# Expert layers: sorted rows turned by tile, up weights stationary in a copied buffer, routing weight applied in the sum

## The chip, the cores and the metric

The kernel runs on one core of a Trainium2 chip. The metric is the device time of one execution in microseconds (us). The kernel before takes 1945.29 us, the median of three runs (1944.04 to 1947.86).

## The reference

One block of four residual layers on x of 4 x 1024 tokens with 128 channels, all float32:

```
x = x + attn_a(layernorm(x))     # 16 heads of 8 channels
x = x + moe(layernorm(x))        # 8 experts, top 2
x = x + attn_b(layernorm(x))     # gated delta rule, a scan over tokens
x = x + moe(layernorm(x))        # the same experts again

moe(x): probs = softmax(x @ gate_w)          # 128 x 8
        top_w, top_i = top_k(probs, 2); top_w = top_w / sum(top_w)
        for e in range(8):
            h = silu(x @ w1[e]) * (x @ w3[e])   # w1, w3: 128 x 256
            out += route[:, e] * (h @ w2[e])    # w2: 256 x 128
```

The change is to the moe alone, which the kernel runs twice.

## The kernel before

`moe` sorts the 4096 tokens by their pair of experts (28 pairs) and works through the sorted rows in tiles of 128. A *pass* is one tile with one expert. A tile meets two experts and more where a pair ends inside it, so that 2 x 32 + 27 = 91 passes (`NPASS`) always suffice; those not needed get addresses of a zero weight. One layer goes as follows.

**Routing** (DVE, with small tables made by POOL). `find_best` takes each token's two experts, `count_pairs` counts the pairs, `place_all` gives each token its place in the sorted order (`slot`), and `plan` gives each pass the first row of its tile (`row_at`) and the place of its expert's weights in SBUF (`w_at`). ScalarE meanwhile writes the normalised rows into `xr` (L1144). Each row of `xr` has 144 numbers: 128 channels, the routing weight of each of 8 experts, and the token's number.

**Scatter.** POOL issues 32 indirect DMAs (L1064), each of which writes 128 rows of `xr` to their sorted places in DRAM (`expert_rows`). They wait for `xr`, for the weights and for `slot`. `plan` runs beside them.

**The 91 passes.** SP loads the tile of each pass from DRAM (L1025), one DMA of 72 KB for each pass, into one of eight buffers (`xin`). Each engine has its own order, written out by hand, and waits on semaphores:

- PE, for pass n: `up(n)` (L1095) is one float32 matmul with the turned tile stationary and 512 columns of w1 and w3 moving; its output has tokens on the partitions. Then PE loads a register with the weights' address for the next pass (L1117). `turn_h(n-2)` (L1102) turns the two halves of the product, `turn_rows` (L1088) in every other pass turns the tiles of the next two passes, and `down(n-3)` (L1110) is two matmuls with w2 moving, summed in PSUM.
- ScalarE: `silu(n)` (L1154), and `take_h(n-2)` (L1159), which copies the turned product to SBUF.
- DVE: `product(n)` (L1311) multiplies silu, the other half and the routing weight; in every other pass `take_rows` (L1295) copies two turned tiles to SBUF and `own_weights` (L1301, L1304) picks the weights out of the rows; `add(n-3)` (L1319) loads a register with the tile's column (L1315) and adds the pass's output to `y`.

In the trace a float32 matmul shows as two records of LDWEIGHTS and two of MATMUL, a transpose as one of each.

**Return.** POOL issues 32 indirect DMAs (L1071) that add `y` to the residual in DRAM. Tile t's waits until min(2t + 29, 91) passes are added. After the first moe the residual is loaded back and its statistics are taken; the second moe writes the kernel's output, and nothing follows it.

Of the kernel before, what the change touches and what calls it, by code (L numbers as in the profile page):

```python
# [11 lines left out]
BF16 = mybir.dt.bfloat16  # L12
ALU = mybir.AluOpType
# [866 lines left out]
COL_W, COL_ID, ROW = P, P + E, 144  # L880
PIECE = 4
NPIECE = NT // PIECE
NXIN = 8
BACK = 8
WE = 3 * F


def moe(nc, g, ins, scr, phase, layer, norm_next, out=None):

    with ExitStack() as ctx:  # L890
# [11 lines left out]
        first = m.sb("first", [P, NT])  # L902
        lane = m.sb("lane", [P, 1])
        names = m.sb("names", [P, E])
        unit = m.sb("unit", [P, NT * E])
# [14 lines left out]
        slot = m.sb("slot", [P, NT], mybir.dt.uint32)  # L920
# [5 lines left out]
        upper = m.sb("upper", [P, NT, PAIRS])  # L926
        lower = m.sb("lower", [P, NT, PAIRS])
        meet = m.sb("meet", [P, NT, E, E])
        needed = m.sb("needed", [P, NT * E])
        upto = m.sb("upto", [P, NT * E])  # L930
        passed = m.sb("passed", [P, NT * E])
        spot = m.sb("spot", [P, 1])
        tile_no = m.sb("tile_no", [P, 1])
        expert = m.sb("expert", [P, 1])
        none = m.sb("none", [P, 1])
        code = m.sb("code", [P, 2])
        spread = m.sb("spread", [P, 2, P])
        row_at = m.sb("row_at", [P, NPASS], mybir.dt.int32)
        w_at = m.sb("w_at", [P, NPASS], mybir.dt.int32)
        which = m.sb("which", [P, NPASS, E])  # L940
        ids = m.sb("ids", [P, NT, 2], mybir.dt.uint32)
        xin = m.sb("xin", [P, NXIN, ROW])
        mine = m.sb("mine", [P, 2, 2, E])
        scale = m.sb("scale", [P, NPASS])
        xgT = m.sb("xgT", [P, 3, 2 * P])
        gate = m.sb("gate", [P, 3, F])
        hs = m.sb("hs", [P, 3, F])
# [3 lines left out]
        ps_t = m.ps("ps_t", [P, CH])  # L951
        ps_r = m.ps("ps_r", [P, CH])
        ps_g = m.ps("ps_g", [P, CH])
        ps_p = m.ps("ps_p", [P, CH])
        ps_h = [m.ps(f"ps_h{i}", [P, 2, F]) for i in range(2)]
# [9 lines left out]
        s_ids = m.sem("ids_set")  # L965
# [23 lines left out]
        s_hturn = m.sem("h_turned")  # L989
        s_hT = m.sem("hT")  # L990
# [5 lines left out]
        ps_ht = [ps_t, ps_r]  # L996
        ps_up = [*ps_h, ps_p[:, :].rearrange("p (w f) -> p w f", w=2)]
        before, total = ps_p[:, 0:PAIRS], ps_p[:, PAIRS:2 * PAIRS]
        spread_ps = ps_p[:, 2 * P:4 * P]
# [13 lines left out]
        def _(sp):  # L1013
            sp.dma_start(resid_tiles, g.x[:, :, :]).then_inc(s_kept, 16)
            sp.wait_ge(s_scat, landed)
            for n in range(2):
                sp.dma_start(xin[:, n, :], scr.xg[0:P, :]).then_inc(s_load[n], 16)
            sp.wait_ge(s_plan, 1)
            for n in range(2, NPASS):
                if n >= NXIN:  # L1020
                    pair = (n - NXIN) // 2
                    sp.wait_ge(s_gturn, pair + 1)
                    sp.wait_ge(s_mine, pair + 1)
                row = sp.value_load(row_at[0:1, n:n + 1], min_val=0, max_val=(NT - 1) * P)
                sp.dma_start(xin[:, n % NXIN, :], scr.xg[bass.ds(row, P), :]).then_inc(s_load[n % NXIN], 16)  # L1025
                if n == NXIN - 1:
                    sp.dma_start(ids[:, :, :], scr.xg.bitcast(mybir.dt.uint32)[:, COL_ID:COL_ID + 2].rearrange(
                        "(t p) o -> p t o", p=P)).then_inc(s_rid, 16)
# [7 lines left out]
        def _(pool):  # L1036
            pool.iota(rank[:, :], pattern=[[-1, E]], base=E, channel_multiplier=0,
                      allow_small_or_imprecise_dtypes=True).then_inc(s_tables, 1)
            pool.memset(unit[:, :], 1.0).then_inc(s_tables, 1)
            pool.iota(xr[:, :, COL_ID:COL_ID + 1].bitcast(mybir.dt.int32), pattern=[[P, NT], [0, 1]], base=0,  # L1040
                      channel_multiplier=1).then_inc(s_ids, 1)
            pool.memset(xr[:, :, COL_ID + 1:ROW], 0.0).then_inc(s_ids, 1)
# [15 lines left out]

# [1114 lines left out]
```

## Time and profile before

| | |
|---|---|
| runs | 1944.04, 1945.29, 1947.86 us |
| profiled execution | 1948.65 us, span 1946.9 us |
| mean granted TensorE clock | 0.826 |
| busy over the span | PE 68%, DVE 76%, ACT 47%, POOL 17% |
| first moe | from 862.9 us (its first DMA) to its last return DMA at 1082.6 us |
| second moe | from 1720.1 us to the end |
| passes | 925 to 1081 us and 1782 to 1939 us |

The span is the time from the first to the last instruction. The percentages are means over stages of different kinds: the attention fills the first 830 us, the delta rule lies between the two moe layers. For a change to the moe only the stretches of the moe say what it is worth.

### The profile page before, as it was taken

Reading aid. Unit: us, or ns where it says so; the run is one execution under the profiler, and the core shown is the slowest. Engines: PE = TensorE matmul, PEld = TensorE weight load, DVE = VectorE, ACT = ScalarE, POOL = GpSimd, SP = SyncE. Lnnn points to the kernel's source line nnn. Section 1 sums busy time; section 2 is a strip of 40 time slices with the busy share of each in tenths; the row PEclk is TensorE's granted clock in tenths of the full one; section 3 lists DMA queues with packets and bytes.
Section 4 is the critical chain, followed back from the end, with each engine's and each line's share of the span. In section 5 each row is a group of like instructions: output and inputs, shape, how many; then the busy total and the mean of one; then the engine's idle time right before and its main releaser. Section 6 shows DMA issues by size and latency. Waiting matters only on the chain. (4 is left out here: it accounts for less than half of the span.)

```text
span 1946.9 us, 42337 instructions
## 1 busy us (share of the span) xinstructions
PE 1322.8 (68%) x15088; PEld 722.1 (37%) x15088; DVE 1484.1 (76%) x2893; ACT 918.5 (47%) x2025; POOL 328.7 (17%) x330
## 2 busy tenths in 40 slices
PE   4689999999999999960999482000000079923998
PEld 2215555554555555350566242000000024411665
DVE  5698899989998999153566484999999979961665
ACT  4508888888888888951344372001222200030443
POOL 6000000000000000016034100000000045544044
PEclk9859999999999999985899785555555589965999
DMA  3510111111111100031233227610221110012243
GB/s 91 175 46 23 37 30 30 30 30 30 31 39 46 33 3 3 2 109 49 54 62 63 52 106 123 188 44 11 65 66 46 26 49 0 1 57 59 52 67 44
DMA packets 118653, 100.86 MB, mean 52 GB/s; under 512 B 23665, under 2 KB 100018, under 8 KB 118066
## 3 DMA queue, kind: packets, MB, share of 16 engines
q1 hardware_dynamic: 101570, 84.79, 17.0%
q0 software_dynamic: 11264, 8.92, 3.2%
q10 hardware_dynamic: 5616, 4.47, 1.3%
q8 instruction: 124, 2.03, 0.4%
q14 instruction: 79, 0.65, 0.1%
HBM read 55.98 MB, written 31.21 MB: 45 GB/s over the span
## 5 line engine op out<-in xcount | busy, mean ns | idle before, releaser
L727 DVE TENSOR_REDUCE att_negmax<-att_ps_max 128x1 f32<-128x1024 f32 x512 | 620.8, 1223 | 66.1 <-PE att_ps_max L590 37.3
L715 ACT ACTIVATE att_probs<-att_ps_prob 128x512 f32<-128x512 f32 x1024 | 556.3, 595 | 128.8 <-PE att_ps_prob L605 126.4
L590 PE MATMUL att_ps_max<-av_k_op,av_q_op 81*32 81x512 bf16 x4096 | 418.1, 401 | 13.2 <-PEq L104 7.2
L605 PE MATMUL att_ps_prob<-av_q_op,av_k_op 99*32 99x512 bf16 x4096 | 407.7, 382 | 2.9
L625 PE MATMUL att_ps_acc<-att_probs,att_vq 128*32 128x256 f32 x4096 | 313.8, 379 | 0.0
L1942 PE MATMUL out_ps_y<-all_bo_row,all_ones 1*128 1x128 f32 x2 | 0.8, 481 | 372.4 <-PEq L104 372.4
L590 PEld LDWEIGHTS att_ps_max<-av_k_op,av_q_op 81*32 81x32 bf16 x4096 | 112.7, 97 | 145.6 <-DVE att_negmax L727 44.9
L605 PEld LDWEIGHTS att_ps_prob<-av_q_op,av_k_op 99*32 99x32 bf16 x4096 | 108.8, 95 | 145.7 <-ACT att_probs L715 93.8
L625 PEld LDWEIGHTS att_ps_acc<-att_probs,att_vq 128*32 128x32 f32 x4096 | 131.2, 111 | 78.2 <-issue 0.5
L1154 ACT ACTIVATE moe_moe_gate<-moe_moe_ps_h 128x256 f32<-128x256 f32 x122 | 46.7, 383 | 214.1 <-PE moe_moe_ps_h L1095 202.1
L1942 PEld LDWEIGHTS out_ps_y<-all_bo_row,all_ones 1*128 1x128 f32 x2 | 0.5, 304 | 372.7 <-issue 372.7
L1095 PE MATMUL moe_moe_ps_h<-all_w_all,moe_moe_xgT 128*128 x244 | 128.8, 610 | 1.4 <-DVE moe_moe_xgT L1295 1.4
L1319 DVE TENSOR_TENSOR moe_moe_y<-moe_moe_y,moe_moe_ps_y 128x128 f32 x182 | 52.4, 288 | 87.9 <-issue 81.7
L1844 ACT ACTIVATE solve_p<-solve_state,solve_decay 128x32 f32<-128x32 f32 x128 | 45.0, 352 | 155.5 <-DVE solve_state L1828 155.5
L1110 PE MATMUL moe_moe_ps_y<-all_w_all,moe_moe_hT 128*128 x728 | 111.6, 276 | 0.3
L531 POOL CAST att_nm_parts<-att_nm_rows 32x128 bf16<-32x128 f32 x16 | 4.5, 284 | 546.4 <-ACT att_nm_rows L696 546.4
L1110 PEld LDWEIGHTS moe_moe_ps_y<-all_w_all,moe_moe_hT 128*128 128x128 f32 x728 | 95.5, 191 | 1.5 <-issue 1.5
L1295 DVE COPY moe_moe_xgT<-moe_moe_ps_g 128x256 f32<-128x256 f32 x92 | 38.2, 415 | 68.2 <-PE moe_moe_ps_g L1088 68.2
L1937 POOL TENSOR_TENSOR out_qS<-b_q,out_St 128x1024 f32<-128x1024 f32 x32 | 75.4, 2355 | 65.9 <-DVE out_St L2046 65.9
L1088 PE MATMUL moe_moe_ps_g<-all_ident,moe_moe_xin 128*128 128x128 f32 x182 | 36.3, 280 | 68.8 <-DMA moe_moe_xin<-expert_rows 68.7
L1311 DVE SCALAR_TENSOR_TENSOR moe_moe_hs<-moe_moe_gate,moe_moe_scale,moe_moe_ps_h 128x256 f32<-128x256 f32 x122 | 58.3, 478 | 21.9 <-ACT moe_moe_gate L1154 21.7
L2046 DVE TENSOR_TENSOR_SCAN out_St<-b_a,out_ps_k 128x1024 f32<-128x1024 f32 x32 | 73.2, 2287 | 1.1
(276 smaller groups left out, 2067.0 us busy)
## 6 DMA issues: line engine op xcount, KB each, us to landing
moe_moe_xin<-expert_rows SPq DMA_DIRECT2D x182, 72.0 KB
av_k_op<-terms_k SPq DMA_DIRECT2D x48, 216.0 KB
av_q_op<-terms_q SPq DMA_DIRECT2D x144, 72.0 KB
solve_dec_and_windows<-solve_Xw SPq DMA_DIRECT2D x16, 256.0 KB, 3.0
solve_dec_and_windows<-solve_k SPq DMA_DIRECT2D x16, 256.0 KB, 3.7
terms_q<-qkv_parts_q SPq DMA_DIRECT2D x8, 384.0 KB, 2.6
terms_k<-qkv_parts_k SPq DMA_DIRECT2D x8, 384.0 KB, 3.1
all_w_all<-in_f_w SPq DMA_DIRECT2D x24, 128.0 KB, 2.5
```

The lines of the kernel that those rows point to most:

```text
L590: mm = pe.matmul(ps_max[c * STRIP:(c + 1) * STRIP, a % 2, k * CH:(k + 1) * CH], q_op[s][0:R_ALL, h, at:at + STRIP], k_op[s][0:R_ALL, h, k ...
L605: mm = pe.matmul(ps_prob[c * STRIP:(c + 1) * STRIP, j % 2, :], k_op[s][0:R_END, h, at:at + STRIP], q_op[s][0:R_END, h, half * CH:(half + 1 ...
L625: mm = pe.matmul(ps_acc[half][32 * h:32 * h + 32, cols], vq[:, s % 2, kt, VW * h:VW * h + 32], probs[:, (GH * v + h) % PROBS, cols], start ...
L715: act.activation(probs[:, j % PROBS, :], ps_prob[:, j % 2, :], ACT.Exp).then_inc(s_exp, 1)
L727: dve.tensor_reduce(negmax[:, s % 2, a:a + 1], ps_max[:, a % 2, :], AX.X, ALU.max, negate=True).then_inc(s_maxed, 1)
L1095: pe.matmul(ps_up[n % 3][:, :, :].rearrange("p w f -> p (w f)"), xgT[:, n // 2 % 3, cols], wall[:, bass.ds(at0, 2 * F)], start=True, stop= ...
L1110: mm = pe.matmul(ps_y[n % 2][:, 0:P], hT[:, n % 3, i * P:(i + 1) * P], wall[:, bass.ds(at0 + (2 * F + i * P), P)], start=(i == 0), stop=(i ...
L1154: act.activation(gate[:, n % 3, :], ps_up[n % 3][:, 0, :], ACT.Silu).then_inc(s_silu, 1)
L1311: dve.scalar_tensor_tensor(out=hs[:, n % 3, :], in0=gate[:, n % 3, :], scalar=scale[:, n:n + 1], in1=ps_up[n % 3][:, 1, :], op0=ALU.mult, ...
L1319: dve.tensor_tensor(tile, tile, ps_y[n % 2][:, 0:P], ALU.add).then_inc(s_sum, 1)
L1937: pool.tensor_tensor(qS[:, e % 2, :], q[:, b * S:(b + 1) * S], St[:, e % 2, :], ALU.mult).then_inc(s_qS, 1)
L2046: dve.tensor_tensor_scan(St[:, e % 2, :], a[:, tok], ps_k[e % 2][:, :], 0.0, ALU.mult, ALU.add).then_inc(s_S, 1)
```

## The change

Five things are different in `moe`.

1. SP loads the sorted rows once, all 32 tiles, in seven DMAs of 1, 1, 2, 4, 8, 8 and 8 tiles (`PARTS`) into `xs`, which keeps them all. PE turns each tile once and DVE copies each once (`xgT` keeps all 32).
2. `up` has the weights stationary: four float32 matmuls of 128 columns, with 128 x 128 of w1 or w3 stationary and the turned tile moving. Its output has the 256 inner channels on the partitions, so that the product is already in the form that `down` needs: `turn_h`, `take_h` and `hs` go, and `down` follows two passes behind instead of three. ScalarE copies the weights of pass n+3 into one of three buffers (`wbuf`), at an address that it loads into a register of its own.
3. PE and DVE load two registers with one load (`two_loads`), without a check of the bounds at run time. ScalarE's load has the check.
4. The routing weight is no longer in the product. `add` multiplies by it, from `xs` at a column found by register: its form is now `scalar_tensor_tensor`.
5. `plan` is replaced: `experts_of_tiles` works with one tile on each partition, `order_passes` and two groups of eight bf16 matmuls on PE give the addresses, `read_plan` writes them out. `experts_of_tiles` stands ahead of `places`, which gives `slot`. POOL makes more small tables (35 memsets in `incid`), and no longer clears `meet`.

```diff
-            for n in range(2):
-                sp.dma_start(xin[:, n, :], scr.xg[0:P, :]).then_inc(s_load[n], 16)
-            sp.wait_ge(s_plan, 1)
-            for n in range(2, NPASS):
...
-                row = sp.value_load(row_at[0:1, n:n + 1], min_val=0, max_val=(NT - 1) * P)
-                sp.dma_start(xin[:, n % NXIN, :], scr.xg[bass.ds(row, P), :]).then_inc(s_load[n % NXIN], 16)
+            for i, (at, end) in enumerate(zip(PARTS, PARTS[1:])):
+                sp.dma_start(xs[:, at:end, :], scr.xg[at * P:end * P, :].rearrange("(t p) o -> p t o", p=P)
+                             ).then_inc(s_load[i], 16)
...
             def turn_rows(j):
+                pe.wait_ge(s_load[part_of(j)], 16)
                 wait_used(pe, s_gT, j)
...
+                pe.transpose(ps_g[:, j % 4 * P:(j % 4 + 1) * P], xs[:, j, 0:P], g.ident[:, :]).then_inc(s_gturn, 1)
+            def up(n, row):
+                pe.wait_ge(s_gT, min(n // 2 + 1, NT))
+                pe.wait_ge(s_wb, n + 1)
                 wait_used(pe, s_h, n - 2)
-                cols = slice((n % 2) * P, (n % 2 + 1) * P)
-                pe.matmul(ps_up[n % 3][:, :, :].rearrange("p w f -> p (w f)"), xgT[:, n // 2 % 3, cols],
-                          wall[:, bass.ds(at0, 2 * F)], start=True, stop=True).then_inc(s_up, 1)
+                for i in range(2 * MF):
+                    mm = pe.matmul(ps_up[n % 3][:, i * P:(i + 1) * P], wbuf[:, n % 3, i * P:(i + 1) * P],
+                                   xgT[:, bass.ds(row, P)], start=True, stop=True)
+                mm.then_inc(s_up, 1)
...
             for n in range(NPASS):
-                up(n, starts[n])
+                up(n, row)
                 if n + 1 < NPASS:
-                    starts[n + 1] = start_of(n + 1)
+                    row, starts[n + 1] = addresses(n + 1)
                 if n >= 2:
-                    turn_h(n - 2)
-                if n % 2 == 0 and n + 2 < NPASS:
-                    turn_rows(n // 2 + 1)
-                if n >= 3:
-                    down(n - 3, starts.pop(n - 3))
+                    down(n - 2, starts.pop(n - 2))
+                if n % 2 == 0 and n // 2 + 2 < NT:
+                    turn_rows(n // 2 + 2)
...
+            def copy_weights(n, at0):
+                act.activation(wbuf[:, n % 3, :], wall[:, bass.ds(at0, 2 * F)], ACT.Copy).then_inc(s_wb, 1)
...
             for n in range(NPASS):
+                if n + 3 < NPASS:
+                    at0 = start_of(n + 3)
                 silu(n)
-                if n >= 2:
-                    take_h(n - 2)
+                if n + 3 < NPASS:
+                    copy_weights(n + 3, at0)
...
             def add(n):
-                row = dve.value_load(row_at[0:1, n:n + 1], min_val=0, max_val=(NT - 1) * P)
+                at = two_loads(nc, dve_at[0:1, n, :], nc.vector.engine)
+                row, col = bounded(nc, at[0], 0, (NT - 1) * P), bounded(nc, at[1], COL_W, (NT - 1) * ROW + COL_ZERO)
...
-                dve.tensor_tensor(tile, tile, ps_y[n % 2][:, 0:P], ALU.add).then_inc(s_sum, 1)
+                dve.scalar_tensor_tensor(out=tile, in0=ps_y[n % 2][:, 0:P], scalar=xs_flat[:, bass.ds(col, 1)],
+                                         in1=tile, op0=ALU.mult, op1=ALU.add).then_inc(s_sum, 1)
...
+            def experts_of_tiles():
+                dve.wait_ge(s_tables, 4)
+                also(dve.tensor_scalar(upper[:, :], ends[:, :], tile_to[:, 0:1], None, ALU.min))
+                chain.done(dve.tensor_scalar(lower[:, :], base[:, :], tile_from[:, 0:1], None, ALU.max))
+                chain.done(dve.tensor_tensor(meets[:, :], upper[:, :], lower[:, :], ALU.is_gt))
+                dve.wait_ge(s_incid, 1 + E - 1 + PAIRS)
+                chain.done(dve.tensor_tensor(hits[:, :, :], incid[:, :, :],
+                                             meets[:, :].unsqueeze(1).to_broadcast([P, E, PAIRS]), ALU.mult))
+                chain.done(dve.tensor_reduce(needed[:, :], hits[:, :, :], AX.X, ALU.max))
+                dve.tensor_tensor_scan(local[:, :], unit[:, 0:E], needed[:, :], 0.0, ALU.mult,
+                                       ALU.add).then_inc(s_count, 1)
```

## Rows read from the trace of the kernel before

**Rows 1.** Windows, passes of both layers: stretch, length, busy us (instructions) of PE, PEld, DVE, ACT, POOL, clock, DMA.

```profile
935.00:1075.00 140.00, 140.00 (x771) 94.63 (x770) 86.89 (x300) 56.39 (x173) 43.73 (x28) 1.00 0.34 59
1792.00:1932.00 140.00, 140.00 (x771) 94.67 (x770) 87.01 (x300) 56.40 (x173) 43.63 (x28) 1.00 0.35 59
```

**Rows 2.** Chain of waits in steady passes: start, us on the chain, what.

```profile
1831.19 0.86 PE moe_moe_ps_h L1095 x2
1832.05 0.22 PE moe_moe_ps_r L1102 x2
1832.27 0.45 PE moe_moe_ps_y L1110 x4
```

**Rows 3.** Timeline, weight loads of the router, whose matmuls have 8 columns.

```profile
859.83 1.92 PEld L841 LDWEIGHTS oproj_ps_z<-all_gate_c,oproj_xT 128*128 128x128 f32 x16
```

**Rows 4.** Timeline of DVE in two steady passes: start, us, then idle before.

```profile
1832.71 0.47 DVE L1311 SCALAR_TENSOR_TENSOR moe_moe_hs<-moe_moe_gate,moe_moe_scale,moe_moe_ps_h 128x256 f32<-128x256 f32 x1
1833.47 0.29 DVE L1319 TENSOR_TENSOR moe_moe_y<-moe_moe_y,moe_moe_ps_y 128x128 f32 x1 [0.29 <-issue]
1834.03 0.48 DVE L1311 SCALAR_TENSOR_TENSOR moe_moe_hs<-moe_moe_gate,moe_moe_scale,moe_moe_ps_h 128x256 f32<-128x256 f32 x1 [0.28 <-ACT moe_moe_gate L1154]
1834.43 0.42 DVE L1295 COPY moe_moe_xgT<-moe_moe_ps_g 128x256 f32<-128x256 f32 x1
```

**Rows 5.** Timeline of ACT in one steady pass.

```profile
1833.62 0.38 ACT L1154 ACTIVATE moe_moe_gate<-moe_moe_ps_h 128x256 f32<-128x256 f32 x1 [0.87 <-PE moe_moe_ps_h L1095]
1833.90 0.38 ACT L1159 ACTIVATE moe_moe_hT<-moe_moe_ps_t 128x256 f32<-128x256 f32 x1
```

**Rows 6.** PE's sequencer, register load L1117 and addresses L1110: ns min/median/max, starts.

```profile
L1117 PEldq TENSOR_LOAD <-moe_moe_w_at x1: 309/309/309, 1833.4 to 1833.4; - x1
L1117 PEldq FUSED_REGOPS  x1: 151/151/151, 1833.8 to 1833.8; - x1
L1117 PEldq SEQ_ASSERT  x1: 18/18/18, 1834.0 to 1834.0; - x1
L1110 PEldq FUSED_REGOPS  x2: 46/46/46, 1834.3 to 1834.4; - x2
```

**Rows 7.** Groups by line, operations of the forms that the change adds.

```profile
L715 ACT ACTIVATE att_probs<-att_ps_prob 128x512 f32<-128x512 f32 x1024 | 556.3, 595 | 128.8 <-PE att_ps_prob L605 126.4
L2031 DVE SCALAR_TENSOR_TENSOR all_x<-out_ps_y,b_q_scale,all_x 128x128 f32<-128x128 f32 x32 | 8.6, 339 | 7.7 <-PE out_ps_y L1968 7.7
```

**Rows 8.** Timeline of DVE, ACT and POOL ahead of the second layer's scatter.

```profile
1732.32 0.18 DVE L1234 TENSOR_TENSOR moe_moe_base<-moe_moe_ends,moe_moe_ps_p 128x28 f32<-128x28 f32 x1
1732.54 0.21 DVE L1235 TENSOR_TENSOR moe_moe_member<-moe_moe_base,moe_moe_ps_p 128x28 f32<-128x28 f32 x1
...
1737.72 0.18 DVE L1242 TENSOR_SCALAR moe_moe_slot<-moe_moe_slot_f 128x32 uint32<-128x32 f32 x1
...
1739.94 0.39 DVE L1254 TENSOR_TENSOR moe_moe_meet<-moe_moe_upper,moe_moe_lower 128x224 f32<-128x224 f32 x1
...
1730.61 7.78 ACT L1144 ACTIVATE moe_moe_xr<-all_x,all_nmr,all_rstd 128x128 f32<-128x128 f32 x20
...
1739.20 1.61 POOL L1064 DMA_INDIRECT expert_rows<-moe_moe_xr,moe_moe_slot  x1 [11.22 <-ACT moe_moe_xr L1144]
```

**Rows 9.** Timeline of PE, first up, first turn_h and last up of the second layer.

```profile
1785.52 2.07 PE L1095 MATMUL moe_moe_ps_h<-all_w_all,moe_moe_xgT 128*128 x2 [0.70 <-DVE moe_moe_xgT L1295]
...
1791.22 0.52 PE L1102 MATMUL moe_moe_ps_t<-all_ident,moe_moe_hs 128*128 128x128 f32 x2
...
1933.82 1.02 PE L1095 MATMUL moe_moe_ps_h<-all_w_all,moe_moe_xgT 128*128 x2
```

**Rows 10.** Timeline of DVE and POOL at the end of the second layer.

```profile
1936.94 0.29 DVE L1319 TENSOR_TENSOR moe_moe_y<-moe_moe_y,moe_moe_ps_y 128x128 f32 x1 [0.54 <-DVE moe_moe_y L1319]
...
1937.50 1.55 POOL L1071 DMA_INDIRECT out_x<-moe_moe_y,moe_moe_ids  x1 [0.68 <-DVE moe_moe_y L1319]
1939.36 1.56 POOL L1071 DMA_INDIRECT out_x<-moe_moe_y,moe_moe_ids  x1 [0.30 <-issue]
```

More of the change, by code:

```diff
@@ L879, with two_loads, bounded, part_of @@
 NPASS = 2 * NT + PAIRS - 1
-COL_W, COL_ID, ROW = P, P + E, 144
+COL_W, COL_ID, COL_ZERO, ROW = P, P + E, P + 12, 144
 PIECE = 4
 NPIECE = NT // PIECE
-NXIN = 8
+PARTS = [0, 1, 2, 4, 8, 16, 24, 32]
 BACK = 8
 WE = 3 * F
+ONES_AT = 8
+def two_loads(nc, where, engine):
+    _, values = nc.values_load_multi_w_load_instructions(
+        where, engines=[engine], min_val=0, max_val=max(NT * ROW, E * WE),
+        skip_runtime_bounds_check_because="the plan is made of counts that the shapes bound")
+    return values
+def bounded(nc, value, low, high):
+    return nc.s_assert_within(value, low, high,
+                              skip_runtime_bounds_check_because="the plan is made of counts that the shapes bound")
+def part_of(tile):
+    return max(i for i in range(len(PARTS)) if PARTS[i] <= tile)
 def moe(nc, g, ins, scr, phase, layer, norm_next, out=None):
@@ L925, in moe @@
         part = m.sb("part", [P, 2, NT, E])
[L926 to L940, printed above, removed]
+        upper = m.sb("upper", [P, PAIRS])
+        lower = m.sb("lower", [P, PAIRS])
+        meets = m.sb("meets", [P, PAIRS])
+        hits = m.sb("hits", [P, E, PAIRS])
+        needed = m.sb("needed", [P, E])
+        local = m.sb("local", [P, E])
+        prefix = m.sb("prefix", [P, 1])
@@ L971, in moe @@
         s_pos = m.sem("positions")
+        s_count = m.sem("tile_counts")
+        s_prefix = m.sem("tile_prefix")
+        s_turns = m.sem("pass_turns")
+        s_passes = m.sem("passes")
+        s_plan = m.sem("plan")
         s_gap = m.sem("gap")
@@ L1079, in _ @@
             pe.matmul(total, g.ones[:, :], chosen[:, :], start=True, stop=True).then_inc(s_pos, 1)
-            pe.wait_ge(s_code, 1)
-            pe.matmul(spread_ps, g.ones[:, :], spread[:, :, :].rearrange("p i n -> p (i n)"), start=True,
-                      stop=True).then_inc(s_spread, 1)
+            pe.wait_ge(s_count, 1)
+            pe.matmul(ps_prefix, earlier[:, :], local[:, E - 1:E], start=True, stop=True).then_inc(s_prefix, 1)
+            pe.wait_ge(s_turns, 1)
+            pe.wait_ge(s_tables, 9)
@@ L1084, in turn_rows @@
+            for e in range(E):
+                pe.matmul(ps_row, tile_b[:, :], turn_of[:, e, :], start=(e == 0), stop=(e == E - 1))
+            for e in range(E):
+                mm = pe.matmul(ps_exp, exp_b[:, e:e + 1], turn_of[:, e, :], start=(e == 0), stop=(e == E - 1))
+            mm.then_inc(s_passes, 1)
             def turn_rows(j):
+                pe.wait_ge(s_load[part_of(j)], 16)
                 wait_used(pe, s_gT, j)
-                for n in range(2 * j, min(2 * j + 2, NPASS)):
-                    pe.wait_ge(s_load[n % NXIN], 16 * (n // NXIN + 1))
-                    mm = pe.transpose(ps_g[:, (n % 2) * P:(n % 2 + 1) * P], xin[:, n % NXIN, 0:P], g.ident[:, :])
@@ L1170, in _, with also @@
             chain = Count(dve, s_chain)
+            def also(op):
+                op.then_inc(s_chain, 1)
+                chain.n = chain.n + 1
             def spreads():
@@ new lines, in order_passes @@
+            def order_passes():
+                dve.wait_ge(s_prefix, 1)
+                chain.done(dve.tensor_copy(prefix[:, :], ps_prefix))
+                dve.wait_ge(s_count, 1)
+                chain.done(dve.scalar_tensor_tensor(out=upto[:, :], in0=local[:, :], scalar=prefix[:, 0:1],
+                                                    in1=needed[:, :], op0=ALU.add, op1=ALU.mult))
+                dve.wait_ge(s_tables, 5)
+                dve.tensor_tensor(turn_of[:, :, :], order[:, :].unsqueeze(1).to_broadcast([P, E, P]),
+                                  upto[:, :].unsqueeze(2).to_broadcast([P, E, P]), ALU.is_equal).then_inc(s_turns, 1)
```

246 lines of the change are left out of this document (105 added, 141 removed).

## The prediction

> **What bounds the kernel now.** I read the windows first. In both layers, over 140 us of passes, PE is busy 140.00 of 140.00 us at a granted clock of 1.00 of full speed (2.4 GHz), while DVE has 87 and ACT 56 us [rows 1]. A busy PE is a modelled one, so I read the chain of waits next: in steady passes it stays on PE and is made of three pieces, 0.86 us for `up`, 0.22 for the two transposes of `turn_h`, 0.45 for `down` [rows 2]. That is 1.53 us, and in every other pass the two transposes of `turn_rows` add another 0.22, so 1.64 us on average. The pieces follow each other without a gap: the passes are bound by what PE streams. As a test, from the first `turn_h` at 1791.22 to the end of the last `up` (1933.82 + 0.86) are 143.5 us [rows 9]. In them stand 88 `up`, 88 `turn_h`, 44 pairs of `turn_rows` and 87 `down`: 88 x 0.86 + 132 x 0.22 + 87 x 0.45 = 143.9. The terms explain the stretch.
>
> Two more places count. The scatter ahead of the passes starts at 1739.20, when both `slot` (DVE, done at 1737.90) and `xr` (ACT, done at 1738.39) are there [rows 8]; the loads wait for its landing. At the end the last return DMA starts at 1939.36 [rows 10].
>
> **PE's passes.** `up` now has four float32 matmuls of 128 columns, so eight records of LDWEIGHTS and eight of MATMUL. That is the shape of `down`, where four such pairs take 0.45 on the chain, 0.1125 a pair [rows 2]. So `up` costs 8 x 0.1125 = 0.90 instead of 0.86: the same columns stream, cut differently. The weight loads cost next to nothing if they lie beside the matmuls before them. That they take time of their own shows where the matmuls have 8 columns only: 16 loads in 1.92 us, 0.12 each [rows 3]. In `down` a load of 0.12 and a matmul together take 0.1125, so they run side by side.
>
> A rule of the Trainium skill speaks against this: "TensorE: Matmul & The Clock Gate", Part 3, under "What overlaps and what doesn't", has weight loads overlap matmuls in flight only when the row group differs, and all eight here fill all rows. By it the time would be that of the last rival below. In `down` the trace disagrees with it; Part 2 of the same page allows the overlap for a background buffer of weights.
>
> Transposes: `turn_h` goes (88 x 0.22 = 19.4 in the stretch above); `turn_rows` was 44 pairs (9.7) and is now 29 single transposes of 0.11 (3.2). One more `down` falls in the stretch, since it follows two passes behind and not three (0.45). Together: +88 x 0.04 - 19.4 - 9.7 + 3.2 + 0.45 = -21.9 us a layer. The steady pass is then 0.90 + 0.45 + 29/88 x 0.11 = 1.39 us. Since PE still has no gap in it, I see no reason for the clock to leave 1.00.
>
> **Do the others keep up with 1.39 us?**
>
> DVE: from the start of `product` to the start of `add` are 0.76 us, of which DVE is idle 0.29 behind its register load [rows 4]. I keep 0.76, though two checks fewer can only shorten it. `add` has a new form; the nearest row of that form and size takes 0.339, against 0.29 [rows 4, 7]. So 0.76 + 0.34 = 1.10 us. With `take_rows` in between, 0.40 more (product to copy, start to start [rows 4]): 1.50, every other pass, for the first 60. The mean of 1.30 is under 1.39, and the late 0.11 of one pass is taken back in the next, because `down` of the same pass comes two passes later. `own_weights` (two operations every other pass) is gone.
>
> ACT: `silu` 0.38 [rows 5] and the copy of 128 x 512. The trace has no copy of that size from SBUF; from PSUM it takes 0.595 [rows 7], and by [rows 5] 256 columns take 0.38 (0.28 start to start). Bounds 0.45 and 0.75; I take 0.60, the row. That is 0.98 us. Its register load with the check takes, by PE's, 0.65 us (0.31 load, check from 1833.8, end about 1834.05 [rows 6]). It is issued behind the copy of the pass before, and on DVE such a load runs beside the operation issued before it: only 0.29 of its length shows as idle [rows 4]. So it lies beside the copy. All in series would be 1.63 us.
>
> PE's own sequencer: it loads two registers with one load and no check (0.31 to 0.37), has about three waits and three address computations, each some 0.12 apart as the two of L1110 are (1834.3, 1834.4 [rows 6]), and hands on 24 instructions: about 1.1 to 1.2 us, and it works ahead of the array. If the four matmuls of `up` compute their common address four times, 0.36 more: 1.5. The upper bound has the checks too (0.28 for each register): 2.06. I take 1.2, beside the array.
>
> Waits added: `up` waits for `s_wb`. Behind it stand PE's whole order, and for PE wait DVE and ACT. The copy was issued three passes (over 4 us) earlier and takes 0.6, so it is never late in steady state. The first three copies run under the scatter, which lasts 40 us after the plan's start. `down(n-2)` needs `product(n-2)`, and this ends 1.1 us after `up(n-2)`: `silu` starts 0.2 after it, `product` 0.41 later [rows 4, 5]. Two passes are 2.8 us.
>
> DMA: SP's 91 loads become 7, the first two as small as before (72 KB). Tile j is needed at pass 2j - 4, one in 2.8 us; nothing there is late. If the larger ones were slow, the first to show would be tile 2, during the second pass: at most about 2 us once a layer. I count nothing.
>
> **Routing.** `experts_of_tiles` puts six operations ahead of `slot`: four small ones at 0.22 start to start, two of them without a wait behind them (0.12), and two of 224 elements at 0.43 (0.39 and the hand-over) [rows 8]. 2 x 0.22 + 2 x 0.12 + 2 x 0.43 = 1.5 us. `slot` is done at 1739.4 instead of 1737.9 and becomes the later of the two, 1.0 us behind `xr`: +1.0 us a layer. Bounds: 0.3 (if half of them hide in hand-overs) and 3. POOL's 35 small memsets stand ahead of it, but POOL idled 11.22 us before the scatter [rows 8]: covered up to 0.3 us a memset. `order_passes` and `read_plan` run under the scatter, as `plan` did.
>
> **Start and end of the passes.** The first two tiles are turned at the low level of the clock, at which a transpose takes 0.22; one goes before the first `up` and one after it: -0.4. At the end, `turn_h` and `take_h` go from the way of the last product. After the last `up` (1934.68) the add of pass 88 was done at 1937.23, and the last return DMA followed at 1939.36, behind the one before it (1.86 apart) [rows 10]. Now: 0.20 + 0.41 to the start of `product`, 0.76 to `add`, 0.34 for it, 0.27 to POOL (1937.50 - 1937.23), 1.86 to the last: 3.84 instead of 4.68. -0.8.
>
> **Sum.** -21.9 - 0.4 - 0.8 + 1.0 = -22.1 us a layer, -44.2 for the two. The profiled execution (1948.65 us, span 1946.9, 1.75 around it) would come to 1904.5. It was 3.4 above the median of the runs; from that, 1945.3 - 44.2 = 1901 us.
>
> **The rivals.**
>
> *A helper sets the pace.* DVE with `take_rows` (1.50) doesn't recover, or PE's sequencer computes each address (1.5). For it: both numbers lie above 1.39. Against it: DVE's mean is 1.30, and PE's extra addresses are a guess. At 1.50 us a pass, 0.11 x 182 = +20: 1921 us.
>
> *ScalarE in series.* Load, `silu` and copy one after the other, 1.63 us a pass: 0.24 x 182 = +44, so the gain is used up: 1945, no change. Against it: DVE's load beside its operation [rows 4].
>
> *Slower: PE's sequencer.* Its place is between `up` and `down`; its price is the upper bound of 2.06 us a pass: 0.67 x 182 = +122, 2023 us. It makes the kernel slower from 1.39 + 44/182 = 1.63 us a pass. For it: the longest register work of a pass stands on PE, and it has grown. Against it: it takes checks that the diff leaves out.
>
> *Slower: weight loads not hidden.* Eight loads of 0.12 more a pass: 0.96 x 182 = +175, 2076 us. It decides from 0.03 us a load. Against it: `down` [rows 2, 3]. (This is also what the rule of the Trainium skill above would give.)
>
> *The change doesn't do what it says*: the count of passes and tiles is fixed in the code, so the work that goes does go; I give this no chance of its own.
>
> **Chances.** The forecast (1890 to 1913) 0.74. A helper sets the pace (1913 to 1938) 0.15. Faster than 1890 0.03: PE's pairs would have to take 0.107 and no more. ScalarE in series or another way to no gain 0.02. Slower 0.06 (sequencer 0.04, weight loads 0.02). A measurement of this kernel tells 0.2% (3.9 us) from no change. Faster: 0.74 + 0.15 + 0.03 = 0.92; same 0.02; slower 0.06. The range 1890 to 1927 leaves out 0.03 below, and above it 0.05 of the helpers and 0.08 of the rest.
>
> **What would show it.** In the changed profile the chain of the passes should have `up` at 0.90 with 8 records and `down` at 0.45, no other piece but 0.11 in every other pass, up to pass 58; the windows should show PE at 100% and the clock at 1.00; a pass 1.41 us in the first 60 and 1.35 after. ACT should have 0.3 us and more idle a pass, waiting for PE. The scatter should wait for DVE's `slot`, 1.0 us later after the layer's start. The forecast is wrong if PE's weight loads show idle time that "issue" or DVE ended, if the windows of the passes show the clock under 1.00, or if the 91 passes take over 135 us.

## The result, and the profile after

| | us |
|---|---|
| before, same chip (4 runs) | 1946.57 median, 1944.04 to 1949.06 |
| changed (4 runs) | 1899.24 median, 1898.65 to 1899.49 |
| ratio | 0.9755, 95% interval 0.9741 to 0.977 |
| profiled execution | 1899.49, span 1897.8, mean clock 0.824 |
| second `moe`, its first POOL instruction to its last return DMA | 219.2 before, 195.3 after |
| first `moe`, the same | 219.7 before, 196.2 after |

The kernel is 47.3 us faster; 1901 us was predicted. The two layers account for 47.4 us (23.5 and 23.9), so nothing outside them is needed to explain it.

The window view of the second layer's passes answers to [rows 1] (length, busy us of PE, PEld, DVE, ACT, POOL, then the clock):

```profile
1765.00:1885.00 120.00, 120.00 (x1077) 120.00 (x1077) 72.82 (x203) 78.46 (x174) 45.22 (x29) 1.00 0.22 27
```

PE is as full as before, at the same clock; the passes are bound by what it streams, and it streams less. The chain of waits, which answers to [rows 2], says what is left of a pass:

```profile
1802.24 0.89 PE moe_moe_ps_up L1123 x8
1803.13 0.45 PE moe_moe_ps_y L1131 x4
...
1804.92 0.11 PE moe_moe_ps_g L1116
```

`turn_h` is gone, a turned tile costs 0.11 in every other pass, and `up` takes 0.89. The groups by line show that the weight loads of the new `up` lie beside its matmuls: 1456 loads of 196 ns, and 0.1 us of idle time before them in the whole kernel.

```profile
L1123 PEld LDWEIGHTS moe_moe_ps_up<-moe_moe_xgT,moe_moe_wbuf 128*128 128x128 f32 x1456 | 181.4, 196 | 0.1
```

They are only just hidden. The windows show PEld busy 120.00 of 120 us too, where it had 94.6 of 140 [rows 1]. With 8 columns to stream beside it a load takes 0.12 [rows 3], and a load with 128 columns takes 0.89 / 8 = 0.111 here. By these two numbers fewer than 128 moving columns would cost as much as 128; no run here tests that.

The timelines of DVE and ACT in two passes (start, us, the idle time before and what ended it) answer to [rows 4, 5]:

```profile
1800.26 0.35 DVE L1337 SCALAR_TENSOR_TENSOR moe_moe_y<-moe_moe_ps_y,moe_moe_xs,moe_moe_y 128x128 f32 x1 [0.29 <-issue]
1800.80 0.42 DVE L1328 TENSOR_TENSOR moe_moe_hT<-moe_moe_gate,moe_moe_ps_up 128x256 f32<-128x256 f32 x1 [0.18 <-PE moe_moe_ps_y L1131]
1801.58 0.35 DVE L1337 SCALAR_TENSOR_TENSOR moe_moe_y<-moe_moe_ps_y,moe_moe_xs,moe_moe_y 128x128 f32 x1 [0.36 <-issue]
```

```profile
1800.38 0.39 ACT L1181 ACTIVATE moe_moe_gate<-moe_moe_ps_up 128x256 f32<-128x256 f32 x1 [0.55 <-PE moe_moe_ps_up L1123]
1800.66 0.62 ACT L1173 ACTIVATE moe_moe_wbuf<-all_w_all 128x512 f32 x1
1801.72 0.38 ACT L1181 ACTIVATE moe_moe_gate<-moe_moe_ps_up 128x256 f32<-128x256 f32 x1 [0.44 <-PE moe_moe_ps_up L1123]
```

From the start of the product to the start of the add are 0.78 us on DVE, and both engines end some of their idle time by waiting for PE: they keep up. PE's load of two registers (ns min/median/max), where [rows 6] had 309 for one:

```profile
L891 PEldq TENSOR_LOAD <-moe_moe_pe_at x2: 532/535/538, 1799.8 to 1801.4; - x2
```

Ahead of the scatter, the timeline of DVE and POOL, which answers to [rows 8]; the wait is now for DVE, as forecast:

```profile
1713.98 0.18 DVE L1284 TENSOR_SCALAR moe_moe_slot<-moe_moe_slot_f 128x32 uint32<-128x32 f32 x1
...
1715.00 1.68 POOL L1088 DMA_INDIRECT expert_rows<-moe_moe_xr,moe_moe_slot  x1 [12.03 <-DVE moe_moe_slot L1284]
1716.98 0.97 POOL L1088 DMA_INDIRECT expert_rows<-moe_moe_xr,moe_moe_slot  x1 [0.30 <-issue]
```

The first passes and the end, which answer to [rows 9, 10]:

```profile
1759.10 0.47 PE L1116 MATMUL moe_moe_ps_g<-all_ident,moe_moe_xs 128*128 128x128 f32 x1 [41.42 <-DMA moe_moe_xs<-expert_rows]
...
1760.39 2.05 PE L1123 MATMUL moe_moe_ps_up<-moe_moe_xgT,moe_moe_wbuf 128*128 x8
...
1765.26 0.61 PE L1131 MATMUL moe_moe_ps_y<-all_w_all,moe_moe_hT 128*128 x4
...
1886.40 0.35 DVE L1337 SCALAR_TENSOR_TENSOR moe_moe_y<-moe_moe_ps_y,moe_moe_xs,moe_moe_y 128x128 f32 x1 [0.36 <-issue]
...
1890.22 1.56 POOL L1095 DMA_INDIRECT out_x<-moe_moe_y,moe_moe_ids  x1 [0.30 <-issue]
```

### The profile page after: what moved, and what is told of

Read it like the earlier page. It is cut to its first block and busy times, and to the rows that moved or that the text cites. A ratio compares the mean times of both kernels' runs of the same rounds, so it can differ in the third digit from the quotient of the medians.

```text
span 1897.8 us, 41781 instructions
## 1 busy us (share of the span) xinstructions
PE 1272.3 (67%) x15730; PEld 780.1 (41%) x15730; DVE 1438.5 (76%) x2659; ACT 963.9 (51%) x2025; POOL 327.9 (17%) x408
## 5 line engine op out<-in xcount | busy, mean ns | idle before, releaser
L590 PE MATMUL att_ps_max<-av_k_op,av_q_op 81*32 81x512 bf16 x4096 | 423.1, 401 | 13.2 <-PEq L104 7.2
L605 PE MATMUL att_ps_prob<-av_q_op,av_k_op 99*32 99x512 bf16 x4096 | 412.3, 382 | 2.8
L1123 PE MATMUL moe_moe_ps_up<-moe_moe_xgT,moe_moe_wbuf 128*128 x1456 | 196.6, 279 | 0.0
L1123 PEld LDWEIGHTS moe_moe_ps_up<-moe_moe_xgT,moe_moe_wbuf 128*128 128x128 f32 x1456 | 181.4, 196 | 0.1
L625 PEld LDWEIGHTS att_ps_acc<-att_probs,att_vq 128*32 128x32 f32 x4096 | 135.5, 111 | 75.6 <-issue 1.0
L1181 ACT ACTIVATE moe_moe_gate<-moe_moe_ps_up 128x256 f32<-128x256 f32 x182 | 70.0, 385 | 165.9 <-PE moe_moe_ps_up L1123 159.0
L1173 ACT ACTIVATE moe_moe_wbuf<-all_w_all 128x512 f32 x182 | 113.3, 622 | 14.5 <-issue 14.4
L1337 DVE SCALAR_TENSOR_TENSOR moe_moe_y<-moe_moe_ps_y,moe_moe_xs,moe_moe_y 128x128 f32 x182 | 63.9, 351 | 62.8 <-issue 60.4
L1328 DVE TENSOR_TENSOR moe_moe_hT<-moe_moe_gate,moe_moe_ps_up 128x256 f32<-128x256 f32 x182 | 76.7, 421 | 43.2 <-PE moe_moe_ps_y L1131 31.8
L1323 DVE COPY moe_moe_xgT<-moe_moe_ps_g 128x128 f32<-128x128 f32 x64 | 18.2, 284 | 82.0 <-issue 80.7
```

What stands on the lines that cost most here:

```text
L590: mm = pe.matmul(ps_max[c * STRIP:(c + 1) * STRIP, a % 2, k * CH:(k + 1) * CH], q_op[s][0:R_ALL, h, at:at + STRIP], k_op[s][0:R_ALL, h, k ...
L605: mm = pe.matmul(ps_prob[c * STRIP:(c + 1) * STRIP, j % 2, :], k_op[s][0:R_END, h, at:at + STRIP], q_op[s][0:R_END, h, half * CH:(half + 1 ...
L625: mm = pe.matmul(ps_acc[half][32 * h:32 * h + 32, cols], vq[:, s % 2, kt, VW * h:VW * h + 32], probs[:, (GH * v + h) % PROBS, cols], start ...
L1123: mm = pe.matmul(ps_up[n % 3][:, i * P:(i + 1) * P], wbuf[:, n % 3, i * P:(i + 1) * P], xgT[:, bass.ds(row, P)], start=True, stop=True)
L1173: act.activation(wbuf[:, n % 3, :], wall[:, bass.ds(at0, 2 * F)], ACT.Copy).then_inc(s_wb, 1)
L1181: act.activation(gate[:, n % 3, :], ps_up[n % 3][:, 0:F], ACT.Silu).then_inc(s_silu, 1)
```

## The experiments

Eleven runs of ten kernels; each ratio is against the kernel before on the same chip. Beside the time I read the length of both `moe` layers in the profile of each, from the start of POOL's memset of `moe_y` to the start of the last return DMA, summed over both. It leaves out what the other stages do from run to run; the changed kernel's two profiles differ by 1.0 us in it. The steady pass of the changed kernel is 1.395 us as long as tiles are turned (up to pass 58) and 1.34 after, and the adds of the second layer are 1.36 apart on average.

| kernel | us, median (runs) | ratio, 95% interval | both layers, us |
|---|---|---|---|
| before | 1946.57 (4) | | 430.2 |
| changed | 1899.24 (4) | 0.9755, 0.9741 to 0.977 | 382.4 |
| changed, again | 1897.72 (5) | 0.9747, 0.9734 to 0.976 | 381.4 |
| dummy transposes | 1938.59 (4) | 0.9956, 0.994 to 0.9973 | 421.1 |
| tile stationary | 1932.25 (4) | 0.9922, 0.9906 to 0.9939 | 415.4 |
| two loads on PE | 2004.17 (2) | 1.0293, 1.0272 to 1.0315 | 486.0 |
| two loads on DVE | 1942.61 (8) | 0.9985, 0.9974 to 0.9997 | 426.9 |
| copy twice | 1899.85 (2) | 0.9757, 0.9737 to 0.9778 | 382.7 |
| copy three times | 1977.10 (2) | 1.0156, 1.0138 to 1.0175 | 459.2 |
| slots first | 1896.40 (5) | 0.9753, 0.9738 to 0.9769 | 378.5 |
| dummy matmuls | 1895.72 (5) | 0.9747, 0.9733 to 0.9761 | 377.6 |
| both | 1892.23 (5) | 0.9726, 0.9712 to 0.9739 | 375.0 |
| both, again | 1892.40 (5) | 0.9722, 0.9709 to 0.9736 | 375.6 |

**Two dummy transposes a pass.** Two 128-column transposes of `hT`, into a spare bank that nobody reads, stand in `down`, in the place of the removed `turn_h`.

```diff
             def down(n, at0):
                 pe.wait_ge(s_h, n + 1)
                 wait_used(pe, s_sum, n - 1)
+                for i in range(MF):
+                    pe.transpose(ps_d[:, i * P:(i + 1) * P], hT[:, n % 3, i * P:(i + 1) * P], g.ident[:, :])
```

> The changed kernel, with two transposes of the product added before each down, into a PSUM bank that nobody reads: what turn_h did on PE, and nothing else of it. Theory (PE's array sets the pace, 1.38 us a pass): 2 x 0.11 x 91 x 2 layers = +40 us, 1939 us. Rival (PE had slack, and what was gained came from DVE's and ACT's lighter order): under +10 us.

Measured: 1938.6, 39.4 more than the changed kernel, for 182 x 0.22 = 40. The chain has the new piece and no other:

```profile
1801.69 0.22 PE moe_moe_ps_d L1132 x2
1801.90 0.45 PE moe_moe_ps_y L1134 x4
```

The passes cost what PE streams: 38.7 us in the two layers and 39.4 in all, where the columns account for 40.

**The tile stationary again.** `up` goes back to one matmul of 512 weight columns with the turned tile stationary; `turn_h` and `take_h` come back, `down` follows three behind. Loading and turning each tile once, the routing, the double register loads and the weight in the add stay. ScalarE still makes a copy, of 128 columns.

```diff
-                for i in range(2 * MF):
-                    mm = pe.matmul(ps_up[n % 3][:, i * P:(i + 1) * P], wbuf[:, n % 3, i * P:(i + 1) * P],
-                                   xgT[:, bass.ds(row, P)], start=True, stop=True)
-                mm.then_inc(s_up, 1)
+                pe.matmul(ps_up[n % 3][:, :], wbuf[:, n % 3, :], wall[:, bass.ds(at0, 2 * F)],
+                          start=True, stop=True).then_inc(s_up, 1)
```

> The changed kernel with the old way round of the up matmul alone: the turned tile stationary (ScalarE copies it, 128 columns, since it needs a fixed address), 512 columns of weights moving, turn_h and take_h back, down three passes behind. Tiles stay loaded and turned once, the weight stays in the sum. Theory: a pass is 0.86 + 0.22 + 0.45 + 0.04 = 1.57 us instead of 1.38, +34 us, and the longer way at the end +0.8 a layer: 1935 us. So the stationary weights would be worth some 36 us and the tiles turned once some 13. Rival (most of the gain is the tiles turned and loaded once): 1905 us or less.

Measured: 1932.3, 33.0 more. The pieces are 0.86, 0.22 and 0.45:

```profile
1801.81 0.86 PE moe_moe_ps_up L1127 x2
1802.66 0.22 PE moe_moe_ps_p L1134 x2
1802.88 0.45 PE moe_moe_ps_y L1142 x4
```

The same columns take 0.86 us in one matmul with two loads and 0.89 in four with eight, so six loads more cost 0.03 and the columns set the length of `up`. The turned-round `up`, with the `turn_h` that it makes needless, brings some 33 of the 47 us. The other 14 belong to what this kernel keeps, and the turns saved in the steady stretch (44 x 0.22 - 29 x 0.11 = 6.5 a layer) are 13 of them; that share is a remainder, not a run of its own.

**Two single loads on PE.** Each of PE's registers is loaded for itself, with its check, as before the change.

```diff
-                at = two_loads(nc, pe_at[0:1, n, :], nc.tensor.engine)
-                return bounded(nc, at[0], 0, (NT - 1) * P), bounded(nc, at[1], 0, (E - 1) * WE)
+                return (pe.value_load(pe_at[0:1, n, 0:1], min_val=0, max_val=(NT - 1) * P),
+                        pe.value_load(pe_at[0:1, n, 1:2], min_val=0, max_val=(E - 1) * WE))
```

> The changed kernel, with PE's two registers loaded one after the other, each with its check. Theory: PE's sequencer now has 1.2 us of work in a pass of 1.38 (the double load alone 0.54); with two single loads of 0.65 each it has 1.9, more than the array, and becomes the bound: 0.52 x 182 = +95 us, 1994 us, slower than the kernel before. Rival (the sequencer works so far ahead of the array that its loads never show): no change.

Measured: 2004.2, slower than the kernel before. The chain of waits has PE idle between `up` and `down` in one pass and a round over DVE in the next, 3.99 us for the two (1870.48 to 1874.47). PE's array starts `down` 1.24 us after `up` (1871.18 to 1872.42), where it needs 0.89 for `up`, and `down` itself takes 0.71 instead of 0.45:

```profile
1870.48 0.71 PE moe_moe_ps_y L1131 x4
1871.18 0.89 PE moe_moe_ps_up L1123 x8
1872.08 0.35 issue
1872.42 0.71 PE moe_moe_ps_y L1131 x4
...
1874.47 0.71 PE moe_moe_ps_y L1131 x4
```

The windows show PE's array no longer full; the bound is its sequencer, the part that loads registers and hands on instructions:

```profile
1860.00:1960.00 100.00, 82.76 (x622) 73.24 (x622) 44.20 (x120) 45.67 (x102) 32.74 (x21) 1.00 0.16 15
```

2.0 us a pass against the 2.06 that the prediction gave as the price of a sequencer with all its checks, and (2.0 - 1.395) x 182 = 110 against 105 measured (over all passes the adds are 1.94 apart for 1.36, which makes 104). That rival was real; what kept it away is one load of two registers without a check, and the edit undoes both together. In its trace each single load takes 0.30, its address or bounds work 0.15 and its check 0.02:

```profile
L1139 PEldq TENSOR_LOAD <-moe_moe_pe_at x4: 299/304/310, 1869.0 to 1874.8; - x4
L1139 PEldq FUSED_REGOPS  x4: 151/151/151, 1869.3 to 1875.2; - x4
L1139 PEldq SEQ_ASSERT  x4: 18/18/18, 1869.5 to 1875.5; - x4
```

**Two single loads on DVE.**

```diff
-                at = two_loads(nc, dve_at[0:1, n, :], nc.vector.engine)
-                row, col = bounded(nc, at[0], 0, (NT - 1) * P), bounded(nc, at[1], COL_W, (NT - 1) * ROW + COL_ZERO)
+                row = dve.value_load(dve_at[0:1, n, 0:1], min_val=0, max_val=(NT - 1) * P)
+                col = dve.value_load(dve_at[0:1, n, 1:2], min_val=COL_W, max_val=(NT - 1) * ROW + COL_ZERO)
```

> VectorE's two registers per pass are read by two single loads with their checks, as one kernel before this had for TensorE, instead of by the one load of both. Theory: the loads stand between the product and the weighted add of every pass in VectorE's sequencer, so product-to-add goes from 0.77 to some 1.33 us, and VectorE's pass from about 1.2 to 1.8 us, which is more than TensorE's 1.395: +0.43 us x 182 = +79, about 1978 us, slower than the kernel before. Rival (VectorE's sequencer has that much slack behind TensorE, or reads ahead): no change, 1899.

Measured: 1942.6, 43 us more than 1899.2 (45 by the ratios: (0.9985 - 0.9755) x 1946.6), where 79 were expected: right in kind, wrong in size, and not slower than the kernel before. The timeline of DVE shows why:

```profile
1801.05 0.41 DVE L1328 TENSOR_TENSOR moe_moe_hT<-moe_moe_gate,moe_moe_ps_up 128x256 f32<-128x256 f32 x1
1802.34 0.35 DVE L1337 SCALAR_TENSOR_TENSOR moe_moe_y<-moe_moe_ps_y,moe_moe_xs,moe_moe_y 128x128 f32 x1 [0.88 <-PE moe_moe_ps_y L1131]
1802.60 0.41 DVE L1328 TENSOR_TENSOR moe_moe_hT<-moe_moe_gate,moe_moe_ps_up 128x256 f32<-128x256 f32 x1
1802.93 0.28 DVE L1323 COPY moe_moe_xgT<-moe_moe_ps_g 128x128 f32<-128x128 f32 x1
1803.94 0.35 DVE L1337 SCALAR_TENSOR_TENSOR moe_moe_y<-moe_moe_ps_y,moe_moe_xs,moe_moe_y 128x128 f32 x1 [0.72 <-PE moe_moe_ps_y L1131]
```

From product to add are 1.29 and 1.34, as reckoned, but I had added the copy of the tile to it: it falls in the time of the loads, and the next product starts 0.26 behind the add. A steady pass is 1.60, not 1.81: 0.205 x 182 = 37, where the two layers show 44.5.

The rest is in the same trace. Over the whole second layer the adds are 1.60 apart on average, against 1.36 in the changed kernel, whose late passes are shorter: 0.24 x 180 = 43. Among them are eight passes with 0.35 more each, 2.8 us in the layer, in which DVE's sequencer stands still for some 0.4 at one place or another; why is not shown. The idle time in the timeline is put down to PE, which had long been done at 1802.34: what the add waited for was the register. The chain of waits a few passes on has DVE's register work (DVEq) between product and add, and at 1813.16 one of the eight stops:

```profile
1807.83 0.30 DVEq L1333
...
1808.17 0.18 DVEq L1333
...
1813.16 0.40 issue
```

**The weights copied twice by ScalarE.** A second copy of the same 512 columns, into a buffer that nobody reads.

```diff
             def copy_weights(n, at0):
+                act.activation(wspare[:, n % 3, :], wall[:, bass.ds(at0, 2 * F)], ACT.Copy)
                 act.activation(wbuf[:, n % 3, :], wall[:, bass.ds(at0, 2 * F)], ACT.Copy).then_inc(s_wb, 1)
```

> The changed kernel, with ScalarE's copy of the weights made twice, the first time into a buffer that nobody reads. Theory (ScalarE has 0.44 to 0.55 us idle a pass, its register load lies beside the copy): one copy more is 0.52 to 0.62 us, so it is just over the edge: between +8 and +26 us, 1907 to 1925 us. Rival (load, silu and copy in series): 0.52 more on top of a serial order, over +100 us; and if it costs nothing, ScalarE's idle time was larger than the trace shows.

Measured: 1899.9, so it costs nothing. The expectation failed, and the timeline of ACT says where:

```profile
1782.64 0.38 ACT L1183 ACTIVATE moe_moe_gate<-moe_moe_ps_up 128x256 f32<-128x256 f32 x1
1782.92 0.62 ACT L1174 ACTIVATE moe_moe_wspare<-all_w_all 128x512 f32 x1
1783.44 0.62 ACT L1175 ACTIVATE moe_moe_wbuf<-all_w_all 128x512 f32 x1
1784.09 0.39 ACT L1183 ACTIVATE moe_moe_gate<-moe_moe_ps_up 128x256 f32<-128x256 f32 x1
```

The durations of a pass sum to 1.62, more than PE's 1.395, but the next operation starts 0.10 before the end of the one before: start to start they are 0.28 + 0.52 + 0.52 = 1.32. The register load hides under them. The windows show ACT busy 118.31 of 120 us, and still it holds nobody up:

```profile
1765.00:1885.00 120.00, 120.00 (x1062) 120.00 (x1062) 71.78 (x201) 118.31 (x260) 43.52 (x28) 0.99 0.23 29
```

The Trainium skill, "ScalarE: Activation LUTs", under "What ACT_TABLE_LOAD costs", gives 186 ns and 0.833 ns an element for an ACTIVATE with immediate scale and bias and has neighbours overlap by about 93 ns. An estimate from these figures is 612 ns for 512 columns, and 519 from start to start. The trace agrees with both within 10 ns (622 and 520).

**Three times.** The edit is made once more. This tells the start-to-start reading from the one that ScalarE, three buffers ahead, is off the path for good.

> ScalarE makes its copy of the up weights three times per pass. With two copies it cost nothing, and ScalarE then showed 118 of 120 us busy in the steady stretch; its starts stood 0.28 (gate), 0.52 and 0.52 us (copies) apart, 1.32 us a pass, just under TensorE's 1.34 or 1.45. Theory (what ScalarE costs is the distance from start to start, not the duration of 0.62): a third copy makes its pass 0.28 + 3 x 0.52 = 1.84 us against 1.395, +0.445 us x 182 = +81, about 1980 us. Rival (ScalarE is off the path for good, copies being made ahead by three buffers): 1899.

Measured: 1977.1, 79 more than the changed kernel on the same chip, for 81 expected. The gates start 1.83 apart:

```profile
1850.70 0.50 ACT L1184 ACTIVATE moe_moe_gate<-moe_moe_ps_up 128x256 f32<-128x256 f32 x1
1850.96 0.75 ACT L1174 ACTIVATE moe_moe_wspare<-all_w_all 128x512 f32 x1
1851.48 0.75 ACT L1175 ACTIVATE moe_moe_wspare<-all_w_all 128x512 f32 x1
1852.00 0.75 ACT L1176 ACTIVATE moe_moe_wbuf<-all_w_all 128x512 f32 x1
1852.53 0.50 ACT L1184 ACTIVATE moe_moe_gate<-moe_moe_ps_up 128x256 f32<-128x256 f32 x1
```

The durations have grown to 0.75 while the distance stayed at 0.52. The work is the same, so I read the longer durations as holding some waiting; no run separates the two. Distances are what adds up: 0.28 + 3 x 0.52 = 1.84.

**Slots first.** `experts_of_tiles` is called behind `places`. The write of `member` (line 1262) joins the ordered chain of DVE's operations in return.

```diff
-            experts_of_tiles()
             places()
+            experts_of_tiles()
```

> The DVE operations that list the experts of each tile, which the change put ahead of the slot numbers, are put behind them. Theory: they are the 1.0 us by which the first scatter starts later in each expert layer than before; with them moved back the slots are ready at 1714.2 less about 1.5 us, and the scatter waits for ACT's last normalised rows (done at 1713.28) again. Gain at most 0.9 us a layer, 1.8 us in all: about 1897.5 us. Rival (the scatter's start is hidden behind something else, or the tables then come late for the first pass): no change, 1899, or more.

**Dummy matmuls.** PE is kept busy ahead of the load, from the moment that POOL comes to its last two scatters.

```diff
+                if t == 30:
+                    pool.memset(mark[:, :], 0.0).then_inc(s_warm, 1)
                 pool.indirect_dma_start(...)
...
+            pe.wait_ge(s_warm, 1)
+            for i in range(4):
+                pe.matmul(ps_y[1][:, :], g.ident[:, :], g.w_all[:, 0, 0:CH], start=True, stop=True)
             turn_rows(0)
```

> Four dummy float32 matmuls of 512 columns are put ahead of the first turns of each expert layer, released by a small POOL memset just before the last two tiles are scattered, so that TensorE is busy in the stretch in which it stands idle for some 40 us. Theory (the first passes of a layer run at the lower of the two clock levels because TensorE was idle ahead of them: 4.87 us from the first up matmul to the first down in the changed kernel, against about 2.8 us for the same work at full clock): the first passes run at full clock, 2.1 to 2.6 us less per layer, about -4.5 us in all, so about 1895 us. Rival (TensorE is idle again for the 1 to 2 us of the load and the first turn, and the clock is not granted, or is lost again): no change, 1899, or up to 0.4 us more for the memset ahead of the scatter.

**Both.**

> Both edits, the dummy matmuls and the slots first. Theory: they are at different places of the path (one ahead of the scatter, one behind the load), so their gains add: about -6.3 us, 1893 us. Rival (one of them does nothing): 1895 to 1899.

Each alone is too small to be told by its time: 0.9753 and 0.9747 stand among the 0.9755 and 0.9747 of the changed kernel. Their traces do show them. With the slots first the scatter waits for ACT again, 14.63 us after the memset of `moe_y` instead of 15.54, and the first scatter takes 1.05 where it took 1.68, which nobody forecast and which I can't explain:

```profile
1712.60 1.05 POOL L1088 DMA_INDIRECT expert_rows<-moe_moe_xr,moe_moe_slot  x1 [11.12 <-ACT moe_moe_xr L1165]
```

That is 1.5 us a layer in the second (0.9 of it forecast), and the two layers are 3 to 4 us shorter together (378.5 against 381.4 and 382.4). For the dummies, the timeline of PE in the second run of both edits:

```profile
1748.13 5.68 PE L1150 MATMUL moe_moe_ps_y<-all_w_all,all_ident 128*128 128x512 f32 x8 [33.30 <-POOL moe_moe_mark L1091]
1753.67 0.33 PE L1120 MATMUL moe_moe_ps_g<-all_ident,moe_moe_xs 128*128 128x128 f32 x1
...
1754.79 1.15 PE L1127 MATMUL moe_moe_ps_up<-moe_moe_xgT,moe_moe_wbuf 128*128 x8
...
1755.89 1.95 PE L1127 MATMUL moe_moe_ps_up<-moe_moe_xgT,moe_moe_wbuf 128*128 x16
1757.68 0.61 PE L1135 MATMUL moe_moe_ps_y<-all_w_all,moe_moe_hT 128*128 x4
```

From the first `up` to the first `down` are 2.89 us instead of 4.87: the first passes ran at 2.4 GHz. All six layers with dummies have 2.88 or 2.89; the six of the changed kernel, its second run and the slots first have 4.3 to 5.5, since the clock rises a little earlier or later. The windows over the 8 us around the first turn show it, the changed kernel first (clock 0.53), then both edits (0.80):

```profile
1757.00:1765.00 8.00, 5.33 (x25) 5.00 (x26) 1.39 (x5) 1.50 (x4) 0.00 (x0) 0.53 0.83 153
```

```profile
1749.00:1757.00 8.00, 7.43 (x29) 4.22 (x28) 1.18 (x4) 0.92 (x3) 1.19 (x2) 0.80 0.49 140
```

The dummies took 5.2 to 6.4 us in these layers. In the second layer of the run with them alone they took 6.37, and the first turn stood 4.8 us behind the start of the last scatter, where it stands 4.2 in the changed kernel: they ran into the load's landing and gave back 0.6 us there.

> The changed kernel itself, unchanged, beside the next one: 1899 us, or as many microseconds off that as the kernel before is off 1946.6 on this chip.

> The kernel with both edits (dummy matmuls ahead of the load, slots first) beside the changed kernel on the same chip. Its earlier time stood at 0.9726 of the kernel before, against 0.9755 for the changed kernel, each with some 0.0013 of uncertainty. Theory: it is the faster by the sum of the two gains, 4 to 6 us. Rival (the distance was one of chips): equal within 2 us.

Side by side on one chip: 1897.72 (1896.56 to 1901.6) and 1892.40 (1890.76 to 1894.19), 5.3 us less, and the ranges don't touch; the layers show 5.8. In the layers both edits together (375.0 and 375.6) stand 2 to 3.5 us below either alone (378.5, 377.6), so each does something. With both edits the kernel stands at 0.9722 (0.9709 to 0.9736) of the kernel before.

## Why the prediction was right

- **PE's passes** (-21.9 a layer). From the first `down` (1765.26) to the end of the last `up` (1886.3) are 121.1 us against 143.5: -22.4. `up` is 0.89 and not 0.90, which over 88 passes is 0.9 less; the terms of the old stretch overshot it by 0.4 (143.9 for 143.5), and that takes some of it back. That the stretch is bound by PE's columns is shown by the dummy transposes; that the new `up` is the larger part, by the kernel with the tile stationary.
- **Weight loads.** They are hidden, as `down` had said [rows 2, 3]. The rule of the Trainium skill ("TensorE: Matmul & The Clock Gate", Part 3, "What overlaps and what doesn't") that loads overlap only between row groups does not hold here: eight loads that show 0.196 us each, all filling all rows, stand in an `up` of 0.89.
- **DVE** (0.76 to the add, 0.34 for it) has 0.78 and 0.35. Right; the two single loads show that it would have been the bound at 1.60 without the double load.
- **ACT** (0.60 for the copy) has 0.62; right as a duration. Its series of 1.63 a pass was a rival made of durations; the copies made twice and three times show that ScalarE's pass is 0.28 + 0.52 = 0.80, and the rival was never near.
- **PE's sequencer** (1.2 us, the bound 2.06). The verdict was right, one term too small: its load of two registers takes 0.535, not the 0.31 to 0.37 taken from the row of one. The four matmuls of `up` compute one address between them (182 address computations on L1123 for 182 passes). With two checked loads of 0.65 for the one of 0.54 it sets the pace at 2.0, which leaves 2.0 - 0.76 = 1.24 for the changed kernel, an estimate close to the 1.2. So this helper had 0.15 us to spare.
- **Routing** (+1.0). The last operation on the slots starts 19.05 us after the layer's first instruction instead of 17.55 (+1.5, as summed), and the scatter 20.07 instead of 19.03: +1.0.
- **Start** (-0.4). Too small by 1.4 in the second layer. From the first `up` to what follows the third (`down` now, `turn_h` before) are 4.87 us for 5.70: -0.8. Of this 0.2 is the turn of one tile for two. The rest is that PE reached 2.4 GHz within the second and third `up` (2.98 us for both, where one at the low level takes 1.8), while the kernel before ran three at the low level. That is partly luck: in the first layer the same stretch has 5.47 for 5.71. From the last scatter to the first `up` are 5.45 us for 5.92, -0.5, of which 0.2 was the other forecast turn. And from the first scatter to the last are 39.9 us for 40.4, another -0.5: in the kernel before the third scatter takes 1.52 us where its neighbours take 0.96. Nothing was counted there, and the cause is open.
- **End** (-0.8). From the end of the last `up` to the last return DMA 3.9 for 4.7: -0.8.

The sum: -22.4 + 1.0 - 0.8 - 0.5 - 0.5 - 0.8 = -24.0 a layer, where 23.9 are measured in the second and 22.1 were forecast. The first layer gained 23.5. The forecast was 3 us too cautious for the whole, most of it ahead of the passes and in the first three of them, and the errors nearly all went the same way.

## What to carry to other kernels

When a profile shows one engine full and the chain of waits never leaves it, price a change by the columns that it streams (here with 128 columns or more behind each weight load), and then ask of each helper for its pass from start to start, its sequencer's loads among them: two of the helpers here were one register load away from using up all of the gain (PE) or nearly all of it (DVE). A busy share near 100% is no bound by itself (ACT, 118 of 120 us, cost nothing), and one of 83% can be (PE behind its sequencer). An edit worth one or two microseconds is shown by its own stretch of the trace and by adding it to another, not by its time alone.

## What the runs showed of the hardware

- A load of two registers takes 0.535 us and one of a single register 0.30; with the bounds and the check a single one costs 0.30 + 0.15 + 0.02 on PE and the steps between them, in all about 0.65 ([rows 6], and the two single loads on PE).
- ScalarE starts a copy of 128 x 512 float32 every 0.52 us, though each shows 0.62, or 0.75 when it has no pause.
- Float32 matmuls of 128 columns with a new stationary operand each: 0.111 us for a load and a matmul, at 2.4 GHz.
- After 33 to 42 us without work PE ran its first matmuls at 1.2 GHz; 5.2 to 6.4 us of dummy work just ahead put the first passes at 2.4 GHz, in six layers of six.
